# Routing weights carried by the scattered rows, applied where expert results leave PSUM, and gathers that add to the residual

## The reference, cut to what matters

```
x = x + cross_attention(layernorm(x), ctx)          # x: 4 x 512 x 512 float32
xt = layernorm(x)                                   # 2048 tokens
scores = softmax(xt @ Wg.T)                         # 16 experts
keep the best 2 of 4 expert groups by their largest score
topi = the 4 best experts among them;  weights = scores[topi]
expert_out = (silu(xt @ W1[e].T) * (xt @ W3[e].T)) @ W2[e].T      # inner size 352
y = sum over the 4 chosen experts of weights * expert_out
z = shared feed-forward of inner size 704 = two halves of 352
return x + y + z
```

## Time and profile before

| what | value |
| --- | --- |
| three timed runs | 919.63, 923.56, 924.39 us |
| span of the profiled execution | 919.3 us (its time outside the span is not recorded) |
| PE busy | 899.9 us, 98% |
| DVE, ACT, POOL busy | 557.9, 332.0, 494.3 us |
| shared first half, routed tiles, shared second half | about 240 to 343, 343 to 815, 815 to 917 us of the span |
| 64 scatters, 64 gathers issued by POOL | 62.6 and 67.7 us |
| 64 weighted additions on DVE | 47.6 us |

### The profile page before, as it was taken

The page is one execution under the profiler, slowest core; times in us unless marked ns, Lnnn a source line. Parts: engine busy times, 40 slices in busy tenths (PEclk is TensorE's granted clock), DMA queues, the critical chain, the costliest instruction groups (busy, mean ns, idle before and its releaser), DMA issues.

```text
span 919.3 us, 19365 instructions
## 1 busy us (share of the span) xinstructions
PE 899.9 (98%) x4962; PEld 806.1 (88%) x4963; DVE 557.9 (61%) x1105; ACT 332.0 (36%) x708; POOL 494.3 (54%) x346
## 2 busy tenths in 40 slices
PE   8999998899989999999999999999999999999998
PEld 5777887687889999999999999999999999989997
DVE  6656767888896644544444444444444444459997
ACT  4556554354324322333333333333333333332221
POOL 1127777874167764434646664456666643136772
PEclk9999999999999999999999999999999999999999
DMA  6829996665569956878778776788777755588984
GB/s 214 264 106 385 388 403 251 230 189 172 184 227 297 308 206 207 243 205 247 245 235 252 248 246 203 237 244 258 248 251 249 248 170 158 163 231 241 275 254 144
DMA packets 180649, 218.97 MB, mean 238 GB/s; under 512 B 56576, under 2 KB 124160, under 8 KB 180224
## 3 DMA queue, kind: packets, MB, share of 16 engines
q1 hardware_dynamic: 118080, 123.49, 41.9%
q0 software_dynamic: 20816, 79.44, 26.1%
q10 hardware_dynamic: 41712, 15.54, 6.3%
HBM read 127.38 MB, written 91.03 MB: 238 GB/s over the span
## 4 chain that ended last, share of the span: by engine, by line
PE 80%; DVE 9%; issue 4%; ACT 3%; DMA 3%; ACTq 0%; DVEq 0%; POOL 0%; SPq 0%; POOLq 0%
PE ps L1170 15%; PE ps L1171 15%; PE ps L1172 15%; PE ps L1222 8%; PE ps L1224 8%; PE ps L1223 8%; PE ps L1019 2%; PE ps L1035 2%; PE ps L966 1%; DVE st L1469 1%; DVE res L1467 1%; PE ps L1055 1%; PE ps L1057 1%; PE ps L1056 1%; DVE st L1284 1%
## 5 line engine op out<-in xcount | busy, mean ns | idle before, releaser
L1170 PE MATMUL ps<-whi,xhi 128*128 (+1 forms) x888 | 288.8, 325 | 1.2 <-issue 0.6
L1172 PE MATMUL ps<-whi,xlo 128*128 (+1 forms) x888 | 286.7, 323 | 0.0
L1171 PE MATMUL ps<-wlo,xhi 128*128 (+1 forms) x888 | 286.7, 323 | 0.0
L1544 DVE TENSOR_TENSOR hrow<-ps,sg 128x352 f32<-128x352 f32 x95 | 49.7, 523 | 214.1 <-ACT sg L838 214.1
L1170 PEld LDWEIGHTS ps<-whi,xhi 128*128 128x128 f32 x888 | 167.7, 189 | 6.1 <-issue 1.3
L1171 PEld LDWEIGHTS ps<-wlo,xhi 128*128 128x128 f32 x888 | 167.7, 189 | 3.9
L1172 PEld LDWEIGHTS ps<-whi,xlo 128*128 128x128 f32 x888 | 167.3, 188 | 0.0
L838 ACT ACTIVATE sg<-ps 128x352 f32<-128x352 f32 x111 | 51.5, 464 | 268.1 <-PE ps L1172 268.0
L845 ACT ACTIVATE xhi<-ps 128x512 fp32r<-128x512 f32 x112 | 66.9, 597 | 145.8 <-DVE ps L1505 145.7
L566 POOL TENSOR_TENSOR wlo<-raw,whi 128x2816 fp32r<-128x2816 f32 x16 | 100.7, 6291 | 2.4 <-POOL whi L564 0.9
L658 POOL DMA_INDIRECT raw<-yslot_d,sloti x64 | 67.7, 1058 | 57.7 <-DMA yslot_d<-ysb 22.6
(11 more groups left out here) (201 smaller groups left out, 1583.4 us busy)
## 6 DMA issues: line engine op xcount, KB each, us to landing
raw<-wexp_in POOLq DMA_DIRECT2D x18, 2176.0 KB, 11.1
xslot_d<-zero SPq DMA_DIRECT2D x10, 2048.0 KB, 21.6
xg<-xslot_d SPq DMA_DIRECT2D x320, 64.0 KB, 2.8
yslot_d<-ysb SPq DMA_DIRECT2D x80, 256.0 KB, 2.4
h_d<-hrow ACTq DMA_DIRECT2D x79, 192.0 KB, 3.0
hblk<-h_d SPq DMA_DIRECT2D x79, 192.0 KB, 2.5
xg<-xn_d SPq DMA_DIRECT2D x128, 64.0 KB, 3.7
xq<-x_in SPq DMA_DIRECT2D x16, 256.0 KB, 3.3
```

What stands on the lines that cost most here:

```text
L1170: pe.matmul(ps[:, bank, 0:INTER], xh, wh, start=(k == 0), stop=False)
L1171: pe.matmul(ps[:, bank, 0:INTER], xh, wl, start=False, stop=False)
L1172: mm = pe.matmul(ps[:, bank, 0:INTER], xl, wh, start=False, stop=(k == KT - 1))
```

## The change

The softmax over all 16 experts is computed early (`prob`, one exponential on ACT, then a sum, a reciprocal and a product on DVE). Its 16 floats are appended to each row of `scat`, so a scattered row has 528 floats (`SROW`). In the routed phase SP loads these 16 columns of each slot tile into `wslot`, ACT reads the tile's expert number from the order table, and `y_evac` multiplies by the column of that expert. The gathers write no buffer: each one is a DMA with `compute_op=ALU.add` straight onto `x1`. Two gathers onto the same tile may not be in flight together, so POOL goes through four tiles for k = 0, then the same four for k = 1, and so on, and waits ahead of each for the one before on that tile. `combine`, `gath`, `comb`, `LAG` and `PACE` are gone, and `add_last` waits for all four gathers of its tile.

The diff, cut to its core:

```
...
+SROW = D + E
...
             for c in range(NR // 8):
                 sp.dma_start(xslot_d[c * 8 * P:(c + 1) * 8 * P, :].rearrange("(p r) n -> p r n", p=P),
-                             zero[:, None, :].to_broadcast([P, 8, D])).then_inc(zeroed, 16)
+                             zero[:, None, :].to_broadcast([P, 8, SROW])).then_inc(zeroed, 16)
...
-                sp.dma_start(scat[:, r, :], rows(xn_d, t)).then_inc(scat_loaded[r], 16)
-
-            pipeline(sp, NT, [(XG, next_tile), (3, load_scat)], ring=XG)
+                sp.dma_start(scat[:, r, 0:D], rows(xn_d, t)).then_inc(scat_loaded[r], 16)
+                if type(t) is not int or t >= XR:
+                    sp.dma_start(scat[:, r, D:SROW], prob[:, bass.ds(t, 1), :]).then_inc(scat_loaded[r], 16)
+                elif t == XR - 1:
+                    sp.wait_ge(rt_prob, 1)
+                    for i in range(XR):
+                        sp.dma_start(scat[:, i, D:SROW], prob[:, i, :]).then_inc(scat_loaded[i], 16)
+
+            pipeline(sp, NT, [(XG, next_tile), (3, load_scat)], ramp=4, ring=XG)
...
+            def load_w(t, r, turn):
+                if type(t) is int and t == NR - 1:
+                    return
+                if type(t) is not int or t >= XG:
+                    sp.wait_ge(y_out, 2 + NT + t - XG + 1)
+                sp.dma_start(wslot[:, r, 2:2 + E], rows(xslot_d, t)[:, D:SROW]).then_inc(w_loaded[r], 16)
...
-            stream(sp, [(NR, True, [(-1, load_h), (XG + 1, load_slots), (-3, store_y)], None),
-                        (NT, False, [(0, None), (XG + 1, load_tile(NT + NR, xn_d)), (-4, store_out)], None)], XG)
+            stream(sp, [(NR, True, [(-1, load_h), (XG + 1, load_slots), (-3, store_y), (1, load_w)], None),
+                        (NT, False, [(0, None), (XG + 1, load_tile(NT + NR, xn_d)), (-4, store_out), (0, None)], None)], XG)
...
-                pool.wait_ge(scat_loaded[t % XR], 16 * (t // XR + 1))
+                pool.wait_ge(scat_loaded[t % XR], 32 * (t // XR + 1))
...
-            for t in range(NT):
-                if 1 <= t < GR:
-                    pool.wait_ge(gathered[t - 1], 16 * TOPK)
-                if t >= GR:
-                    pool.wait_ge(mm1, 2 + NT + NR + t - 2)
-                    pool.wait_ge(comb, TOPK * (t - GR + 1))
+            for first in range(0, NT, GR):
                 for k in range(TOPK):
-                    pool.indirect_dma_start(
-                        out=gath[:, t % GR, k, :], out_offset=None, in_=yslot_d,
-                        in_offset=bass.IndirectOffsetOnAxis(ap=sloti[:, t * TOPK + k:t * TOPK + k + 1], axis=0)).then_inc(gathered[t % GR], 16)
+                    for t in range(first, first + GR):
+                        if first or k:
+                            pool.wait_ge(gathered[t % GR], 16 * TOPK * (t // GR) + 16 * k)
+                        pool.indirect_dma_start(
+                            out=x1[:, t, :], out_offset=None, in_=yslot_d,
+                            in_offset=bass.IndirectOffsetOnAxis(ap=sloti[:, t * TOPK + k:t * TOPK + k + 1], axis=0),
+                            compute_op=ALU.add).then_inc(gathered[t % GR], 16)
...
+            act.wait_ge(rt_low, 1)
+            act.activation(prob[:, :, :], prob[:, :, :], ACT.Exp).then_inc(rt_exp, 1)
...
-            def y_evac(t, p, half):
+            words = []
+
+            def load_words(j):
+                words[:] = [act.value_load(packed[0:1, bass.ds(j, 1)], min_val=0, max_val=32 ** XG - 1)]
+
+            def expert(t, r):
+                if type(t) is int:
+                    return act.value_load(order[0:1, t:t + 1], min_val=2, max_val=E + 1)
+                return words[0] // 32 ** ((r + 2) % XG) % 32
+
+            def y_evac(t, r, turn):
+                p, half = r % 2, 2 * turn + r // 2
+                if type(t) is int and t == 0:
+                    act.wait_ge(rt_done, 1)
                 act.wait_ge(mm2, NT + t + 1)
                 if type(t) is int and t == NR - 1:
                     act.wait_ge(y_out, 2 + NT + t)
@@ -895,7 +923,8 @@
                     return
                 if type(t) is not int or t >= 2:
                     act.wait_ge(y_stored[p], 16 * half)
-                act.activation(ysb[:, p, :], ps[:, 5 + p, :], ACT.Copy).then_inc(y_out, 1)
+                act.wait_ge(w_loaded[r], 16 * (turn + 1))
+                act.activation(ysb[:, p, :], ps[:, 5 + p, :], ACT.Identity, scale=wslot[:, r, bass.ds(expert(t, r), 1)]).then_inc(y_out, 1)
...
-            def exponents(t, p, half):
-                if type(t) is int and t == 5:
-                    act.wait_ge(rt_low, 1)
-                    act.activation(score[:, :, :], score[:, :, :], ACT.Exp).then_inc(rt_exp, 1)
-                    act.activation(top8f[:, :, 0:TOPK], top8f[:, :, 0:TOPK], ACT.Exp).then_inc(rt_exp, 1)
+            def silu_again(t, p, half):
+                if type(t) is int and t == 0:
+                    act.activation(silu_warm[:, :], const[:, C_EPS:C_EPS + 1], ACT.Silu).then_inc(warm, 1)
...
-                first = top8[:, :, 0:1]
-                step(dve.tensor_tensor(score[:, :, :], logits[:, :, :], first.to_broadcast([P, NT, E]), ALU.subtract))
-                dve.tensor_tensor(top8f[:, :, 0:TOPK], top8[:, :, 0:TOPK], first.to_broadcast([P, NT, TOPK]), ALU.subtract).then_inc(rt_low, 1)
-
-            def r_weights():
-                dve.wait_ge(rt_exp, 2)
-                step(dve.tensor_reduce(total[:, 0, :], score[:, :, :], AX, ALU.add))
+                dve.tensor_tensor(prob[:, :, :], logits[:, :, :], top8[:, :, 0:1].to_broadcast([P, NT, E]), ALU.subtract).then_inc(rt_low, 1)
+
+            def r_softmax():
+                dve.wait_ge(rt_exp, 1)
+                step(dve.tensor_reduce(total[:, 0, :], prob[:, :, :], AX, ALU.add))
                 step(dve.reciprocal(total[:, 1, :], total[:, 0, :]))
-                step(dve.tensor_tensor(top8[:, :, 0:TOPK], top8f[:, :, 0:TOPK], total[:, 1, :, None].to_broadcast([P, NT, TOPK]), ALU.mult))
+                dve.tensor_tensor(prob[:, :, :], prob[:, :, :], total[:, 1, :, None].to_broadcast([P, NT, E]), ALU.mult).then_inc(rt_prob, 1)
...
+            r_shifted()
             dve.wait_ge(h_pad, 1)
...
             x_turn(0)(2, 2, 0)
-
-            issued = {"comb": 0, "y_out": 2 + NT}
...
-                if issued["comb"]:
-                    dve.wait_ge(comb, issued["comb"])
+                dve.wait_ge(gathered[r], 16 * TOPK * (turn + 1))
...
-            def combine(quarter):
-
-
-                def fn(s, r, turn):
-                    begin, end = (max(0, min(TOPK * NT, ((4 * u + v) - 4 * LAG) * PACE // 8)) for u, v in ((s, quarter), (s, quarter + 1)))
-                    for n in range(begin, end):
-                        t, k = n // TOPK, n % TOPK
-                        if k == 0:
-                            dve.wait_ge(gathered[t % GR], 16 * TOPK * (t // GR + 1))
-                        dve.wait_ge(y_out, issued["y_out"])
-                        if n:
-                            dve.wait_ge(comb, n)
-                        dve.scalar_tensor_tensor(x1[:, t:t + 1, :], gath[:, t % GR, k:k + 1, :], top8[:, t:t + 1, k],
-                                                 x1[:, t:t + 1, :], ALU.mult, ALU.add).then_inc(comb, 1)
-                        issued["comb"] += 1
...
```

More of the change, by code:

```diff
@@ L219, in xattn_moe @@
             wr_sb = sb2("wr_sb", [P, KT, E], F32)
-            zero = sb2("zero", [P, D], F32)
+            zero = sb2("zero", [P, SROW], F32)
             st1 = sb2("st1", [P, 2, 6], F32)
@@ L243, in xattn_moe @@
         score = sb3("score", [P, NT, E], F32)
+        prob = sb3("prob", [P, NT, E], F32)
         total = sb3("total", [P, 2, NT], F32)
@@ L257, in xattn_moe @@
         ysb = sb3("ysb", [P, 2, D], F32)
-        scat = sb3("scat", [P, XR, D], F32)
+        scat = sb3("scat", [P, XR, SROW], F32)
         hhi.append(sb3("hhi_odd", [P, IC * P], F32R))
@@ L262, in xattn_moe @@
         hblk = sb3("hblk", [P, XG, IC * P], F32)
+        wslot = sb3("wslot", [P, XG, 2 * E], F32)
+        silu_warm = sb3("silu_warm", [P, 1], F32)
         wo_sb = raw[:, 1, 0:KT * D].rearrange("p (k n) -> p k n", k=KT)
         gate_gamma, gate_beta = head_in[:, 0, 2 * S:3 * S], head_in[:, 0, 3 * S:4 * S]
-        gath = raw[:, :, :].rearrange("p a n -> p (a n)")[:, 0:GR * TOPK * D].rearrange("p (r k n) -> p r k n", r=GR, k=TOPK)
         ps = psum("ps", [P, 8, 512], F32)
@@ L271, in xattn_moe @@
         xn_d = nc.dram_tensor("xn_d", [TOK, D], F32, kind="Internal").ap()
[L272 removed]
+        xslot_d = nc.dram_tensor("xslot_d", [NR * P, SROW], F32, kind="Internal").ap()
         yslot_d = nc.dram_tensor("yslot_d", [NR * P, D], F32, kind="Internal").ap()
@@ L305, in xattn_moe @@
         xn_stored = [sem(f"xn_stored{r}") for r in range(XR)]
-        rt, rt_low, rt_exp, rt_sel, rt_mm, rt_slots, rt_done = (sem(n) for n in ("rt", "rt_low", "rt_exp", "rt_sel", "rt_mm", "rt_slots", "rt_done"))
```

(15 more changed lines are left out.)

14 lines of the change are left out of this document (3 added, 11 removed).

## The result

| | before | changed |
| --- | --- | --- |
| timed runs, median | 923.48 us (919.63 to 924.39) | 938.48 us (937.75 to 942.74) |
| ratio, 95% interval | 1 | 1.018 [1.015, 1.021] |
| span of the profiled execution | 919.3 us | 936.4 us |
| PE busy | 98% | 96% |

The account below looks back on a forecast made before the run. The prediction took PE, busy almost without gaps, to set the time in every stage touched. Its terms, 0 + 0.3 + 0.2 + 8.4 = 8.9 us, on the median of 923.56 gave 932.5 us, range 920 to 948.

Parts of the forecast that it names:

- Part 1: Shared second half: removing DVE's 64 weighted additions gains 0 to 5.4 us; taken as 0.
- Part 2: Early softmax on DVE, ACT and SP ahead of the first tiles: +0.3 us, bounds -0.5 to +2.
- Part 3: Routed phase: longer rows, one more small SP load a tile, scaled copy on ACT: +0.2 us, bounds 0 to +2.
- Part 4: Shared second half: 16 dependent rounds of gathers make tile 12 late, delaying the end by 8.4 us.
- R: Time of one round of four dependent gathers: taken as 7.4 us, low end 5.2, high end 8.7.
- 16R - 110.0: Delay of the end: tile 12 complete at 799.9 + 16R against 909.87, its `add_last`'s latest free start; 8.4 us.
- the prediction's chain: Backwards from tile 15's `down` at 911.64 through `hlo`, `hrow` and `add_last`: latest free start of tile 12's `add_last` 909.87.
- plain price: Rival: an accumulating gather lands as fast as a plain one, round 5.2 to 6.9 us; 924.1 us, chance 0.36.
- Doubled engine time: Rival: accumulating gathers also read `x1`, doubling DMA engine time; round 8.7 us, delay 29.2, time 953, chance 0.14.
- Late evacuation: Rival: register read and wait for `w_loaded` on ACT make `hhi` late; at most 2 us, 926, chance 0.07.
- DVE's relief: Rival: without DVE's additions PE waits less for `hlo` and `hlo_odd`; at most about 3 us, 920.5, chance 0.05.

Follow-up runs that it names:

- e4_noadds: The kernel before without DVE's 64 weighted additions, `add_last` waiting for its tile's gathers: 921.2 us, ratio 0.9988.
- e3_front: The changed kernel with plain gathers into the old ring, the old pacing and 64 unweighted DVE additions put back: 926.43 us, ratio 1.0043.
- e11_pad716: The changed kernel with plain gathers (addition left out) and a POOL memset of 128x716 floats ahead of each: 932.36 us, ratio 1.0120.
- e2_flag: The kernel before with `compute_op=ALU.add` on its gathers, old order and DVE's additions kept: 955.74 us, ratio 1.037.

## Why the prediction was right, and where it was off

The forecast, 932.5 us by late gathers of tile 12, had the sign, the place and more than half of the size (8.9 us for 15). Point by point:

- *Part 1, DVE's additions*: 0 taken, and -0.1% [-0.4%, +0.1%] measured (e4_noadds).
- *Part 2, the early softmax*: 0.3 taken. It fitted the idle time it was put in:

```profile
247.91 0.38 DVE L1681 TENSOR_REDUCE total<-prob 128x16 f32<-128x256 f32 x1
248.32 0.25 DVE L1682 RECIPROCAL total<-total 128x16 f32<-128x16 f32 x1
248.60 0.42 DVE L1683 TENSOR_TENSOR prob<-prob,total 128x256 f32<-128x256 f32 x1
249.02 0.52 DVE L1523 TENSOR_TENSOR hx<-ps,sg 128x352 f32<-128x352 f32 x1
```

  Between matmuls 1,201 and 1,861 PE lost nothing (-0.1 us against before).
- *Part 3, rows, small loads and scale*: this step failed. 0.2 was taken with an upper bound of 2, and it cost 4 (e3_front). The scale is cheap (693 ns a tile for 605, hidden). What was missed is the entry of the phase: it was judged by means over 380 steady us, while at 354 to 357 us SP issues without pause. The step asked what ACT's and the steady DMA's slack was, and not what is queued behind the new loads in SP at the one place where its queue is full.
- *Part 4, the gathers*: the mechanism held (the table above). The round was 7.7 us for 7.4 taken, the delay 13.8 for 8.4 in the first profile, 11.6 in the second. The mis-sized term is R: its low end, 5.2 us, took POOL's issue at 0.95 us over from the plain gather, and nothing below 7.4 was possible once an issue cost 1.55 (four steps of 1.85). That 7.4 was also the value taken is chance; it had been reached from landings. The table counts the last round by its landing, and not as a sixteenth full one: 16R - 110.0 gives 7.4 for e11_pad716, where 3.9 to 5.3 was measured. For the changed kernel's first profile it gives 13.8 with the measured round, and hits the measured delay by luck: it counts 1.0 us too much for the last round and leaves out 1.4 us of the clock. The `down` of the earlier trace rows, and with it the `hlo` in the prediction's chain, is tile 14's and not tile 15's; what waits for tile 12 first is tile 15's transposes just ahead of it.
- *A second cost of the accumulating gathers, left out*: plain DMAs beside them land later. The last slot tile's store of `h_d` and the `hblk` load behind it took 5.39 + 4.43 us to land before and 7.79 + 4.52 in the changed kernel. Over the five profiles with accumulating gathers in the new order the two take 11.7 to 13.3 us, over the eight with plain ones 8.1 to 9.8, and from matmul 4,321 to 4,429 PE loses 0.7 to 2.3 us, where the plain ones lose at most 0.2. It does not add to the end, which tile 12's last landing sets.
- *A term left out*: behind three of its stalls, at the entry and behind the waits for tiles 8 and 12, PE worked at a lower granted clock. Behind the wait for tile 8:

```profile
895.00:900.00 5.00, 4.29 (x17) 4.32 (x18) 2.97 (x6) 0.60 (x1) 4.09 (x4) 0.66 1.03 186
```

```profile
895.95 0.49 PE L1198 MATMUL ps<-wlo,xhi 128*128 128x352 f32 x1
```

  A matmul of 352 columns takes 0.49 us there, 0.32 elsewhere; the granted clock of 0.66 means that a part of the stretch ran at the 1.2 GHz level in place of 2.4. Matmuls 4,801 to 4,861, which follow this stall's first moments, lose 1.4 us more. After the waits of 3.12 us at the entry and 2.75 us at tile 12 in the changed kernel's second profile the clock stayed at 1.00, so a part of the scatter between the two profiles is the clock.
- *Rivals*: plain price falls (e2_flag). Doubled engine time was right in its premise and wrong as the bound: a gather took 0.68 us more of the engines (285.6 less 239.9, less 2.2 for the scatters' longer rows, over 64), 1.57 in the gathers' own stage for 0.89, a ratio of 1.76, but the round was 7.7 and not 8.7. The sum had taken a DMA share of 1 as the limit, and the windows show 1.06. Late evacuation fell (693 ns a tile, and no lateness in the routed phase), and so did DVE's relief.

The premise of the doubled engine time is what the Trainium skill states in "Collectives: The Full Stack", section "The bandwidth ceiling: the fold count and why AG ≠ RS ≠ AR", of collectives on a ring: adding needs two source reads, and ran 1.93 times slower than copying among four ranks. The trace here, of a gather and no ring, agrees in kind, at 1.76 of engine time. Besides that, the issue itself takes POOL 1.63 times as long here, and e11_pad716, which copies this alone, has 5.3 us of the 11.6 to 13.8.

## What to carry to other kernels

Work taken from an engine that nothing waits for was worth nothing here; what its replacement costs is read from the resources it lands on, here POOL's issue time and SP's queue. For a serial chain of DMAs write down the latest moment that costs nothing and the price of one link from each of its parts (issue, transfer, landing), since the delay is zero up to the threshold and grows with every link behind it. Judge an added load by the densest moment of its queue, mostly the entry of a phase, and not by the phase's mean.

## What the runs showed of the hardware

- `compute_op=ALU.add` on an indirect gather of 128 rows of 2 KB into SBUF: issue 1.55 us for 0.95, landing 6.8 for 4.7 to 4.9, and in the trace twice the packets of half the size (8,192 of 2,048 bytes at 196 ns for 4,096 of 4,096 bytes at 223 ns).
- The busy share of the 16 DMA engines can read over 1 (1.06 in 850 to 900), so in a sum of packet times 1 was no ceiling here.
- Reading a scale from an SBUF column, with `Identity` in place of `Copy`, takes a PSUM eviction of 128x512 on ACT from 605 to 693 ns.
- Plain DMAs of 192 KB beside accumulating gathers, in the changed order, land later: a store and a load in a row took 11.7 to 13.3 us, for 8.1 to 9.8 beside plain gathers.
